# A 512-step recurrence inside a fused kernel: scores computed twice, in two layouts, and the gate products split in four

## What is computed

```
def step(h, x_t):                        # 512 steps, h is 4 x 128
    proj = h @ W
    score = einsum('bsh,bh->bs', enc_hiddens, proj)      # 77 keys a batch
    attn = softmax(score, axis=-1)
    context = einsum('bs,bsh->bh', attn, enc_hiddens)
    gx = concatenate([x_t, context]) @ kernel + bias
    gh = h @ recurrent_kernel
    z = sigmoid(xz + hz); r = sigmoid(xr + hr)
    cand = tanh(xh + r * hh)
    return z * h + (1.0 - z) * cand
```

## Time and profile before

| what | value |
|---|---|
| median of 3 runs | 3105.05 us (3101.61 to 3105.86) |
| span of the profiled execution | 3108.8 us |
| the recurrence in it | 996.5 us (first state) to 2985.3 us (last scan): 1989 us for 512 steps |
| PE / DVE / ACT / POOL busy | 88% / 69% / 55% / 32% of the span |

### The profile page before, as it was taken

The page is one execution under the profiler, slowest core; times in us unless marked ns, Lnnn a source line. Parts: engine busy times, 40 slices in busy tenths (PEclk is TensorE's granted clock), DMA queues, the critical chain, the costliest instruction groups (busy, mean ns, idle before and its releaser), DMA issues. The chain is left out here.

```text
span 3108.8 us, 131004 instructions
## 1 busy us (share of the span) xinstructions
PE 2731.3 (88%) x54162; PEld 1800.4 (58%) x54163; DVE 2144.2 (69%) x8143; ACT 1712.7 (55%) x5762; POOL 995.6 (32%) x1992
## 2 busy tenths in 40 slices
PE   7999999887877999898999898999989877777768
PEld 4666666575455555565666565666656544444438
DVE  5666666773433888688888688777868766776653
ACT  4666666533443666576766576666657543333322
POOL 2000000230100666355666355555535311000015
PEclk9999999999878999999999999999999999999989
DMA  4000000000011000010000010000001000000013
GB/s 141 5 5 7 5 5 5 11 1 4 16 37 35 7 14 31 3 38 10 11 10 31 3 44 4 10 7 11 27 3 37 4 3 3 3 4 3 4 45 80
DMA packets 41078, 56.49 MB, mean 18 GB/s; under 512 B 6238, under 2 KB 27688, under 8 KB 40360
## 3 DMA queue, kind: packets, MB, share of 16 engines
q1 hardware_dynamic: 36392, 42.46, 4.3%
q0 software_dynamic: 4096, 5.67, 0.9%
HBM read 42.45 MB, written 5.67 MB: 15 GB/s over the span
## 5 line engine op out<-in xcount | busy, mean ns | idle before, releaser
L2183 POOL TENSOR_TENSOR gru_terms<-gru_states,gru_signs 128x8 f32<-128x8 f32 x512 | 104.2, 203 | 1180.9 <-DVE gru_states L2470 1077.7
L2103 ACT ACTIVATE gru_p<-gru_ps_sg,gru_negmax 128x78 f32<-128x78 f32 x512 | 167.5, 327 | 355.6 <-DVE gru_negmax L2439 350.4
L2107 ACT ACTIVATE gru_th_r<-gru_pre_r 128x32 f32<-128x32 f32 x512 | 118.8, 232 | 406.7 <-DVE gru_pre_r L2450 406.7
L1691 PE MATMUL gru_ps_sg<-ctx_gate_w,gru_p_t 128*4 128x64 f32 x12288 | 268.4, 221 | 0.1
L368 ACT ACTIVATE self_probs<-self_sc,self_negmax 128x512 f32<-128x512 f32 x256 | 174.4, 685 | 166.1 <-DVE self_negmax L425 166.1
L1936 PE MATMUL gru_ps_sg<-score_w,gru_states 128*4 128x78 f32 x4096 | 165.5, 234 | 94.3 <-DVE gru_states L2470 93.4
L2159 POOL TENSOR_SCALAR bg_probs<-bg_probs,bg_arsum 128x256 f32<-128x256 f32 (+2 forms) x192 | 241.0, 1255 | 19.0
L2443 DVE STREAM_TRANSPOSE gru_p_t<-gru_p 128x96 f32<-128x96 f32 x512 | 142.7, 279 | 112.1 <-ACT gru_p L2103 111.9
L2439 DVE TENSOR_REDUCE gru_negmax<-gru_ps_sg 128x1 f32<-128x78 f32 x512 | 121.7, 238 | 135.4 <-PE gru_ps_sg L1936 132.0
L1940 PE MATMUL gru_ps_own<-late,gru_states 128*4 128x128 f32 x4096 | 208.7, 276 | 0.0
L1691 PEld LDWEIGHTS gru_ps_sg<-ctx_gate_w,gru_p_t 128*4 128x4 f32 x12288 | 172.9, 86 | 38.4 <-issue 0.3
(11 more groups left out here) (421 smaller groups left out, 7391.5 us busy)
## 6 DMA issues: line engine op xcount, KB each, us to landing
bg_w<-in_moe_w SPq DMA_DIRECT2D x48, 256.0 KB, 2.9
bg_wa<-in_wqkv SPq DMA_DIRECT2D x24, 192.0 KB, 2.3
moe_w<-in_moe_w SPq DMA_DIRECT2D x16, 256.0 KB, 2.9
best_w_sb<-in_ec_w SPq DMA_DIRECT2D x16, 256.0 KB
cross_scratch<-ctab_raw SPq DMA_DIRECT2D x16, 154.0 KB
cross_outs<-cross_scratch POOLq DMA_DIRECT2D x4, 576.0 KB, 6.1
late<-in_late SPq DMA_DIRECT2D x1, 2269.5 KB
self_w_sb<-in_wqkv SPq DMA_DIRECT2D x8, 192.0 KB, 2.4
```

The source lines that it names most:

```text
L1691: last = pe.matmul(bank[32 * c:32 * c + B, 0:hi - lo], p_t[:, 32 * k:32 * k + B], gate_w[:, k, 96 * c + lo:96 * c + hi], start=k == 0, sto ...
L2103: act.activation(p[:, 0:CTX + 1], ps_s[:, 0:CTX + 1], ACT.Exp, bias=negmax[:, 0:1], accum_out=total[:, 0:1])\
```

## The change

**Tables.** `gate_w` is 4 x 98 columns wide in each chunk k. Two columns of ones for the real keys (`is_key`) stand ahead of the 96 in each column chunk; the constants `GATE_R, GATE_C, GATE_Z, GATE_ALL` are their borders. It takes 9 small DVE instructions in place of 3 to write them.

**A step.**

- Scores (now L1932): the stationary operand is the state's column of batch b, repeated 32 times, so that all 32 partitions of its group hold the same scores. No mask is added.
- New (L1937): 12 products of 4 columns with 32 columns of `score_w` as stationary operand: scores with keys on partitions, `ps_t` (128 x 12). The mask (now L1926, 5 rows, 12 columns) is written into that bank ahead.
- The exponential (now L2102) reads `ps_t` and writes `p_t` (128 x 12), the gate products' stationary operand. It has no row sum and waits for the maximum and for L1937. The buffer p, its transpose and the four products with `spread` are gone.
- Gate products (now L1705): four groups of 12. Totals (2 columns), r (32), candidate (32), z (32). The candidate's wait for the reciprocal, since totals and candidate share a PSUM bank. Banks are dealt out anew: scores, candidate, totals; turned scores, r; own, z.
- DVE: the reciprocal now stands right ahead of pre_r; u waits for the candidate's products; the transpose of z waits for POOL's two instructions, for which the last scan waited before.
- Fillers: three in a step without background, none elsewhere.

**The background's places.** PE has one hook (`after_gates`) in place of two, between z's products and the next step's x products, and x's products wait for pre_z. `down` is one piece of four products. On DVE `before_gates` becomes `after_maximum` and stands between the maximum and the copy of `ps_own`. On ACT, `unit_input` moves to `after_exp`, `square` and `square_qk` to `after_candidate`. `STAGES` has 23 places instead of 16, a unit lives one or two steps longer, and `turn_qk` uses its own half of a bank. On SP, `wo` has semaphores of its own and is loaded one pair later.

The core of the diff:

```diff
+            def after_gates(t):
+                for g, n, m in chunks_at(t, 0):
+                    up(g, n, m)
                 for g, n, m in chunks_at(t, 3):
-                    down(g, n, m, 0)
+                    down(g, n, m)
+                for g, n, m in units_at(t, "turn"):
+                    turn_qk(g, n, m)
...
             for t in range(S):
-                if t:
-                    pe.wait_ge(s_own, t)
+                busy = t and after_gates(t - 1)
+                wait_positive(pe, s_prez, t)
                 wait_positive(pe, s_xt, t // P)
...
-                busy = t and before_scores(t - 1)
-                wait_positive(pe, s_u, t)
-                pe.matmul(ps_s[:, 0:CTX + 1], mask_l, mask_r[:, 0:CTX + 1], start=True, stop=False, skip_group_check=True)
+                pe.matmul(ps_t, mask_l, mask_r, start=True, stop=False, skip_group_check=True)
                 if not busy:
-                    wait_positive(pe, s_prez, t)
-                    for i in range(6):
-                        fill_in(2 * P, ps_tz)
+                    for i in range(3):
+                        fill_in(2 * P, ps_sc)
                 pe.wait_ge(s_h, t + 1)
                 for b in range(B):
-                    last = pe.matmul(ps_s[32 * b:32 * b + B, 0:CTX + 1], state(t), score_w[:, b, 0:CTX + 1], start=False, stop=True,
-                                     tile_position=(0, 32 * b), skip_group_check=True)
+                    last = pe.matmul(ps_s[32 * b:32 * b + 32, :], state(t)[:, b:b + 1].broadcast_to([P, 32]), score_w[:, b, 0:CTX + 1],
+                                     start=True, stop=True, tile_position=(0, 32 * b))
                 last.then_inc(s_score, 1)
+                for k in range(3):
+                    for b in range(B):
+                        last = pe.matmul(ps_t[32 * b:32 * b + 32, B * k:B * k + B], score_w[:, b, 32 * k:32 * k + 32], state(t),
+                                         start=False, stop=True, tile_position=(0, 32 * b), skip_group_check=True)
+                last.then_inc(s_turnedmm, 1)
...
-                after_own(t)
                 pe.wait_ge(s_exp, t + 1)
-                for c in range(4):
-                    last = pe.matmul(ps_t[32 * c:32 * c + B, 0:2], spread, total[:], start=True, stop=True, tile_position=(0, 32 * c))
-                last.then_inc(s_total, 1)
+                gate_products(ps_totals, 0, GATE_R).then_inc(s_total, 1)
+                gate_products(ps_r, GATE_R, GATE_C).then_inc(s_rmm, 1)
+                pe.wait_ge(s_rt, t + 1)
+                gate_products(ps_c, GATE_C, GATE_Z).then_inc(s_cmm, 1)
                 pe.wait_ge(s_own, t + 1)
-                fill_in(P, ps_own)
-                pe.wait_ge(s_pt, t + 1)
-                gate_products(ps_g, 0, 64).then_inc(s_rcmm, 1)
-                pe.wait_ge(s_rt, t + 1)
-                gate_products(ps_z, 64, 96).then_inc(s_zmm, 1)
+                gate_products(ps_z, GATE_Z, GATE_ALL).then_inc(s_zmm, 1)
...
                 act.wait_ge(s_max, t + 1)
-                act.activation(p[:, 0:CTX + 1], ps_s[:, 0:CTX + 1], ACT.Exp, bias=negmax[:, 0:1], accum_out=total[:, 0:1])\
-                   .then_inc(s_exp, 1)
+                act.wait_ge(s_turnedmm, t + 1)
+                act.activation(p_t[:], ps_t, ACT.Exp, bias=negmax[:, 0:1]).then_inc(s_exp, 1)
```

More of the change, by code:

```diff
@@ L1568, in recurrence @@
         PACE = {1: 2, 2: 2, 3: 3}
+        STAGES = {2: {"project": 0, "squares": 0, "take_v": 1, "sums": 1, "scales": 1, "rows": 2, "turn": 2, "take_qk": 4, "scores": 5,
+                      "max0": 6, "exp0": 6, "max1": 7, "exp1": 7, "scale0": 7, "scale1": 8, "probs0": 7, "probs1": 8, "turned0": 7, "turned1": 9,
+                      "values": 9, "take_out": 10, "out": 10, "add": 11},
+                  3: {"project": 0, "squares": 0, "take_v": 1, "sums": 1, "scales": 1, "rows": 2, "turn": 2, "take_qk": 4, "scores": 4,
+                      "max0": 5, "exp0": 5, "max1": 6, "exp1": 6, "scale0": 6, "scale1": 7, "probs0": 7, "probs1": 8, "turned0": 8, "turned1": 9,
+                      "values": 9, "take_out": 10, "out": 11, "add": 12}}
         ATTENTION, GATING, EXPERTS = {1: 0}, {}, {}
@@ L1572, in recurrence @@
                 ATTENTION[g] = EXPERTS[g - 1] + C + (3 if PACE[g] == 2 else 1)
[L1573 to L1579 removed]
+            GATING[g] = ATTENTION[g] + PACE[g] * (U - 1) + (11 if PACE[g] == 2 else 13)
+            EXPERTS[g] = GATING[g] + 5
+        ADDING = 7
         NORMS = [(g, n) for g in (1, 2, 3) for n in "ghi"]
[L1583 removed]
+        FIRST = {n: {"g": GATING[n[0]], "h": EXPERTS[n[0]] + C + 4, "i": EXPERTS[n[0]] + C + (12 if n[0] < 3 else 10)}[n[1]] for n in NORMS}
         tokens = h_cols.rearrange("p (b s) -> p b s", s=S)
@@ L1708, in up, with down @@
                   .then_inc(s_up, 1)
-            def down(g, n, m, half):
+            def down(g, n, m):
                 e, f = m // FC, n % FC
@@ L1717, in down @@
                         pe.wait_ge(s_y, g)
-                for j in (2 * half, 2 * half + 1):
+                for j in range(B):
                     last = pe.matmul(bk_pair[e % 2][:, j * P:(j + 1) * P], hid[:, m % 2, j * P:(j + 1) * P], w2_sb[:, e % RING, f, :],
@@ L1734, in turn_qk @@
                 pe.wait_ge(s_rows, m + 1)
[L1735 to L1739 removed]
+                wait_positive(pe, s_aq, m)
+                wait_positive(pe, s_oe, min(m - 3 if PACE[g] == 2 else m - 2, g * U))
+                if n < 4:
+                    wait_positive(pe, s_add, (g - 1) * U)
                 wait_positive(pe, s_hid, (g - 1) * C)
                 for i in range(2):
[L1742 removed]
+                    last = pe.transpose(qk_turned[:, i * P:(i + 1) * P], rows[:, i * P:(i + 1) * P], ident)
                 last.then_inc(s_qkt, 1)
@@ L1899, in before_scores @@
                     busy = True
+                for j in range(2):
+                    for g, n, m in units_at(t, f"probs{j}"):
+                        turn_probs(g, n, m, j)
+                        busy = True
                 for at, norm in norms_at(t, 4):
@@ L1906, in before_scores @@
                     busy = True
+                for at, g in gating_at(t, 8):
+                    turn_gates(at, g)
+                    busy = True
                 for at, g in gating_at(t, 9):
-                    gate_biases(at, g, 0)
+                    gate_biases(at, g)
                     busy = True
@@ L1938, in _ @@
                 last.then_inc(s_score, 1)
+                for k in range(3):
[3 more added lines that the diff above has]
+                last.then_inc(s_turnedmm, 1)
                 for c in range(4):
-                    last = pe.matmul(ps_own[32 * c:32 * c + B, 0:P], state(t), h_w[:, c, :], start=False, stop=True,
+                    last = pe.matmul(ps_own[32 * c:32 * c + B, :], state(t), h_w[:, c, :], start=False, stop=True,
```

233 lines of the change are left out of this document (99 added, 134 removed).

## The result

| kernel | median | lowest to highest |
|---|---|---|
| before | 3105.45 us | 3101.61 to 3110.28 (4 runs) |
| changed | 3519.95 us | 3509.84 to 3531.24 (4 runs) |

The ratio is 1.134 (95% interval 1.131 to 1.138): **slower by 415 us**. The forecast was slower by 95, within 3125 to 3290. The direction held and the size did not. The profiled execution has a span of 3525.9 us. Its recurrence (first to last scan) takes 2403.8 us, where it took 1982.8 before: 421 us more, which is all of the difference (the two profiled spans differ by 417).

The account below looks back on a forecast made before the run. A busy step was taken to be bound by the PE-DVE-ACT chain and by PE at once. Step changes summed to +91, plus 1 us for tables and 3 for semaphore waits: +95 on 3105, 3200 us, range 3125 to 3290.

Parts of the forecast that it names:

- The chain without background: Scan to scan in a step without background, through PE, DVE and ACT: 3.61 us, 0.15 less than 3.76.
- The bound of the activation: ACT's exponential on 12 columns: 0.27 us taken, between 0.19 and 0.33, which put the step at 3.53 to 3.67.
- The turned products hidden by the maximum: PE's 24 new score passes start over 0.17 us and finish before the maximum releases ACT, with 0.12 to spare.
- Rival B: Turned products' 32-column loads take turns, 0.64 us replacing 0.17, so the exponential starts later: 3390 us; chance 0.08.
- The period of the busy steps, 2.67 + the background's passes: PE's step length with background in one run, wherever above 3.61 us; experts 4.41 against 3.90.
- the sum of +91: Whole recurrence: experts +44, attention of tiles 2, 1 and 3 +34, +18, +22, steps short of background -27 us.
- The 3 us for semaphore waits: PE's turn_qk and project now wait for three or four semaphores each: 3 us, at least nothing, at most +30.
- Rival C: Three fillers instead of seven or eight let PE's clock fall to 1.2 GHz in the 139 last steps: 3440; chance 0.04.
- the sign named for C: A granted clock below 0.9 in the last stretch would show the forecast wrong.
- The range: Total time 3125 to 3290 us, 8 times in 10: 3145 to 3265 widened by half the distance to neighbouring rivals.

Follow-up runs that it names:

- e3: The changed kernel with three more fillers in each step without background: 3541.9 us, ratio 1.140.
- e7_groups_small24: The kernel of e4_two_groups with 24 small products, which nobody reads or waits for, behind z's products in every step: 3526.2 us, ratio 1.139.
- e2_two_chunks: The changed kernel without the third key chunk (keys 64 to 76) in the turned scores and gate products: 3164.9 us, ratio 1.019.
- e4_two_groups: The changed kernel with two groups of gate products in place of four (totals with r, candidate with z): 3022.66 us, ratio 0.974.

## Why the prediction missed

- **The chain without background.** Right: 3.61 forecast, 3.67 measured, each link within 0.03. The bound of the activation held too: 0.27 us at 12 columns, the value taken.
- **The turned products hidden by the maximum.** Right. 24 passes of 32 stationary columns on four column tiles take 0.35 us in all, some 0.17 of it the last one's length, so they start over 0.18 (0.17 forecast). Rival B did not come about. By the 25 ns between matmuls of the Trainium skill ("TensorE: Matmul & The Clock Gate", section "Wait — 56ns, not 53.3ns?") it would have been 0.60. The measurement decides: that spacing does not hold for passes on four column tiles.
- **The period of the busy steps, 2.67 + the background's passes.** Right within 0.12 us for every kind of step, where it can be seen undisturbed. With the measured lengths the sum of +91 would have become +123. The 3 us for semaphore waits had no row, and no run measured them apart.
- **The step that failed** is the one that is not there. The sum counts the time that passes and instructions take on the engines, and the waits between them. It takes for granted that PE has its next instruction at hand: the arrival of instructions is a term put at nothing without a reason. The change adds 118 instructions in a step without background and 126 in one of experts. The number stood in both listings of the queue and was used for spacing and columns only. Steps of 310 instructions in 4.41 us and of 296 in 3.61 ask for 70 and 82 a microsecond; the runs show 63 to 69. With 67, a step without background takes 4.4 and one of experts 4.6, with the 63 counted there 4.9: 0.7 x 201 + 0.4 x 87 = 175 of the missing 300 us. The rest is in the attention's steps, which are 0.5 to 0.7 over their undisturbed lengths.
- **The granted clock.** Rival C gave 3440 for half clock in the 139 last steps. The clock did fall, in half of that stretch, so the sign named for C came, but e3 shows that the fall cost nothing there. The price was too high as well: a step at 1.2 GHz without a pause takes 4.35 us, 0.7 more than 3.67 and not 1.7. That C's 3440 is nearer to 3520 than the forecast is luck. In the pause shown above the clock fell within the idle time, and a page that shows both invites to explain the pause by the clock.
- **The range** ended at 3290. By its own rule (3265, and half of what lies between it and B's 3390) it should have ended at 3327, and 3520 is outside that too. It had been widened for priced unknowns alone, and the largest one had no name.

The trace of before could have given a warning and no more. In its recurrence the fetches were 5.3 us apart on average, and the closest 5% under 4.1; over ten fetches in a row the most was 54 instructions a microsecond. The change asked for 70 to 82. Its profile can't say what happens at a rate that it never reached, and such a case should get a chance among the rivals.

## What to carry to other kernels

Count the instructions of an engine per microsecond as a resource of its own: where a change turns few large products into many small ones, compare that number with the highest that the trace shows sustained, and give what lies above a price. A pause of TensorE with everything there, between a weight load and its own matmul, with an instruction packet 2 to 3 us ahead of it, is the sign. The test is to put products that nobody reads and nobody waits for into a kernel that runs without pauses (e7_groups_small24), or to take instructions away. If it is the bound, merge groups: the same gate products in half the instructions gave 0.974 of the kernel before, where four groups had given 1.134. Leave clock and order alone until that is done.

## What the hardware showed that I had not expected

- TensorE's instructions arrive in packets of 16 KB, one for some 250 instructions, through the whole execution, and at 64 to 69 a microsecond in the six kernels that asked for more, with 1.8% of the DMA engines' time and granted clocks from 0.69 to 0.92. An fp32 product here is two passes and four instructions, with 2 columns as with 64. The Trainium skill, "Trainium Architecture — The Big Picture", section "The software stack", has the streams copied into the engine when the program is loaded; here 677 packets came during the execution.
- For a few steps PE runs above that rate (296 in 3.67 us is 81 a microsecond), then it pauses for about 1 us. What lies ahead of it in a buffer was not measured, nor why PE goes on only 2.3 to 2.9 us after a packet's start, 1.2 to 1.5 us after its end.
- The clock can be at 1.2 GHz for a long time in all without a pause (e2_two_chunks, 261 of 519 us), while e4_two_groups with the same three fillers and fewer instructions held 0.97. What tells these two apart is open.
